# Second edge sum of a graph network: compare and multiply in one VectorE instruction per tile, in place of wide one-hots and ScalarE copies

## The chip, the cores and the metric

One NeuronCore of a Trainium2 chip runs the whole network in one launch. The metric is the device time of one execution in microseconds (us). The time before is the median of three runs.

## What is computed

The network has 6250 nodes with 256 features and 100000 edges, in two layers. Each layer adds a graph part and a mixer part and then a feed-forward part. The change touches the graph part of the second layer alone, an attention over edges:

```python
h = features @ W_layer.T + b_layer
a1 = (h @ w_a1.T + b_a1)[:, 0]
a2 = (h @ w_a2.T + b_a2)[:, 0]
row, col = indices
v = leaky_relu(a1[row] + a2[col], 0.01)
m = segment_max(v, row, n)
ev = exp(v - m[row])
s = segment_sum(ev, row, n)
out = segment_sum((ev / s[row])[:, None] * h[col], row, n)
```

## The kernel before, in words

The edges have been sorted by the row that they add to and are laid out in 880 tiles of 128 edges. Two tiles form a pair that belongs to one bucket of 128 rows, and 8 tiles (`T8`) form a batch, so that there are 110 batches (`NB`). For each edge `lane` holds its row's number within the bucket (0 to 127). For a tile, the 128x128 matrix with a 1 at (edge, lane of the edge) is its one-hot; multiplied with the gathered rows of `h` on TensorE it adds each edge's row to the right lane.

The class `Messages` holds the work on a batch n, as small functions for each engine:

- GpSimd, `pool_gather`: 8 indirect DMAs fetch the rows of `h` with the score a2 beside them into `g`, a ring of five batches (`GR`). From batch 5 on it waits until TensorE has summed the batch five before.
- VectorE, `dve_hold`: one instruction on 128x1024 elements compares the lane numbers with 0 to 127 and gives the batch's 8 one-hots in `one`, a ring of four. A small instruction on 128x8 then gives the shifted scores `a2s`; it waits for the gathered batch.
- ScalarE, `act_held`: 8 activations on 128x128 (Copy with a scale for each partition) multiply the one-hots by `a2s` and give `held`, of which there is one buffer.
- TensorE, `pe_turn`, two halves: transposes `held` into PSUM. ScalarE, `act_sign`, takes the sign of it (the transposed one-hot, for the lookup below), and VectorE, `dve_peak`, its maximum along the edges.
- VectorE, `dve_chain`: seven small instructions carry the maximum from pair to pair and give the row's m in two bf16 parts. ScalarE, `act_fade`, gives the factor by which the sum so far fades when m rises.
- TensorE, `pe_look`, looks a1 and m up for each edge. VectorE, `dve_exponents`, four small instructions, and ScalarE, `act_exp`, give `ev`.
- VectorE, `dve_weight`: one instruction on 128x1024 multiplies the one-hots in place by `ev`.
- TensorE, `pe_sum`, four pairs, and VectorE, `dve_add`, four times: `acc = acc * fade + sum` at the pair's bucket. The bucket's number is loaded into a register first (L1720), which has four small instructions of its own in VectorE's queue.

`forward_messages` weaves this into the second half of the mixer. Each engine goes through the same steps s; in step s VectorE holds batch s + 2, takes the peaks of batch s + 1, looks up and weights batch s and adds batch s - 1, all in the order that `step` writes out. There are 112 steps. In the first 100, four to a chunk of 250 rows, the mixer's own work on the chunk stands between as `first()` and `second()`; the last 12 hold the edges' work alone. GpSimd has nothing else to do than gather.

The order in VectorE's queue is this (L2067):

```python
            def step(s, first, second):
                ms.dve_hold(dve, s + 2)
                ms.dve_peak(dve, s + 1, 0)
                first()
                ms.dve_add(dve, s - 1, 0)
                ms.dve_add(dve, s - 1, 1)
                ms.dve_peak(dve, s + 1, 1)
                ms.dve_chain(dve, s + 1)
                second()
                ms.dve_exponents(dve, s)
                ms.dve_add(dve, s - 1, 2)
                ms.dve_weight(dve, s)
                ms.dve_add(dve, s - 1, 3)
```

The functions that the change touches, with `forward_messages`, follow.

Of the kernel before, what the change touches and what calls it, by code (L numbers as in the profile page):

```python
# [8 lines left out]
ALU = mybir.AluOpType  # L9
ACT = mybir.ActivationFunctionType  # L10
AX_X = mybir.AxisListType.X
ds = bass.ds
P = 128
# [28 lines left out]
class Phase:  # L42


    def __init__(self, nc, name):
        self.nc, self.name, self.ctx, self.sems = nc, name, ExitStack(), []
        self.loops, self.rings = [], []
# [5 lines left out]
    def sb(self, name, shape, dt=F32):  # L53
        return self.ctx.enter_context(self.nc.sbuf_tensor(f"{self.name}_{name}", shape, dt))
# [4 lines left out]
    def sem(self, name):  # L59
        s = self.nc.alloc_semaphore(f"{self.name}_{name}")  # L60
        self.sems.append(s)
        return s
# [99 lines left out]
PB = 4  # L162
NB = 110
# [1409 lines left out]

LOOK = 6
T8 = 2 * PB
HELD, ONES = 1, 4


class Messages:
# [5 lines left out]
    def __init__(self, nc, held, ctx, order, table_d):  # L1585
        def sb(name, shape, dt=F32, ctx=ctx):
            return ctx.enter_context(nc.sbuf_tensor(f"messages_{name}", shape, dt))
        self.nc, self.order, self.table_d = nc, order, table_d
        self.acc, self.ident, self.bucket = sb("acc", [P, HB, D + 1], ctx=held), sb("ident", [P, P], ctx=held), sb("bucket", [1, NPR], I32)
        self.lane, self.idx = sb("lane", [P, ST]), sb("idx", [P, ST], I32)  # L1590
        with ExitStack() as early:
            self.rec = sb("rec", [P, ST, 3], ctx=early)
        self.g = [sb(f"g{q}", [P, T8, D + 2]) for q in range(GR)]
        self.iota_t = sb("iota", [P, P])
        self.one = [sb(f"one{b}", [P, T8, P]) for b in range(ONES)]
        self.held = sb("held", [P, T8, P])
        self.heldT = [sb(f"heldT{b}", [P, T8, P], BF16) for b in range(2)]
        self.stays, self.a1_c, self.look = sb("stays", [P, NPR]), sb("a1_c", [P, NPR]), sb("look", [P, NPR, LOOK], BF16)
        self.best, self.m, self.shift = sb("best", [P, NPR + 1]), sb("m", [P, NPR + 1]), sb("shift", [P, 2])
        self.a2s, self.peak, self.mraw, self.m32, self.drop, self.fall = ([sb(f"{n}{b}", [P, w]) for b in range(2)] for n, w in (  # L1600
            ("a2s", T8), ("peak", PB), ("mraw", PB), ("m32", PB), ("drop", PB), ("fall", PB)))
        self.fade = [sb(f"fade{b}", [P, PB]) for b in range(3)]
        self.found, self.z, self.lz, self.d, self.ev = ([sb(f"{n}{b}", s) for b in range(2)] for n, s in (
            ("found", [P, T8, 2]), ("z", [P, T8]), ("lz", [P, T8]), ("d", [P, T8]), ("ev", [P, T8])))
        sem = lambda name: nc.alloc_semaphore(f"messages_{name}")
        self.loaded, self.ready = sem("loaded"), sem("ready")
        self.landed = [sem(f"landed{q}") for q in range(GR)]
        (self.onehot, self.shifted, self.held_s, self.hturned, self.signed, self.peaked, self.chained, self.raw, self.maxed, self.m_hi, self.m_mid,
         self.m_sum, self.dropped, self.fallen, self.faded, self.looked, self.read, self.zs, self.lzs, self.less, self.exped, self.weighted, self.summed,
         self.added) = (sem(n) for n in (  # L1610
             "onehot", "shifted", "held_s", "hturned", "signed", "peaked", "chained", "raw", "maxed", "m_hi", "m_mid",
             "m_sum", "dropped", "fallen", "faded", "looked", "read", "zs", "lzs", "less", "exped", "weighted", "summed", "added"))

    def banks(self, ph):
# [24 lines left out]
    def dve_hold(self, dve, n):  # L1639
        if not 0 <= n < NB:  # L1640
            return
        if n == 0:
            dve.wait_ge(self.ready, 2)
        if n >= ONES:
            dve.wait_ge(self.summed, (n - ONES + 1) * PB)
        self.nc.vector.tensor_tensor(self.one[n % ONES][:, :, :], self.iota_t[:, None, :].to_broadcast([P, T8, P]),
                                     self.lane[:, n * T8:(n + 1) * T8].unsqueeze(2).to_broadcast([P, T8, P]), ALU.is_equal).then_inc(self.onehot, 1)
        dve.wait_ge(self.landed[n % GR], (n // GR + 1) * (16 * T8))
        if n >= 2:
            dve.wait_ge(self.held_s, n - 1)  # L1650
        self.nc.vector.tensor_scalar(self.a2s[n % 2][:, :], self.g[n % GR][:, :, D + 1], self.shift[:, 0:1], 1.0, ALU.add, ALU.max).then_inc(self.shifted, 1)

    def dve_peak(self, dve, n, k):
        if not 0 <= n < NB:
# [53 lines left out]
    def dve_weight(self, dve, n):  # L1708
        if not 0 <= n < NB:
            return  # L1710
        one = self.one[n % ONES]
        dve.wait_ge(self.held_s, n + 1)
        dve.wait_ge(self.exped, n + 1)
        self.nc.vector.tensor_tensor(one[:, :, :], one[:, :, :], self.ev[n % 2][:, :].unsqueeze(2).to_broadcast([P, T8, P]), ALU.mult).then_inc(self.weighted, 1)  # L1714

    def dve_add(self, dve, n, k):
        if not 0 <= n < NB:
# [9 lines left out]
                                            ALU.mult, ALU.add).then_inc(self.added, 1)  # L1727

    def act_held(self, act, n):
        if not 0 <= n < NB:
            return
        act.wait_ge(self.onehot, n + 1)
        act.wait_ge(self.shifted, n + 1)
        if n:
            act.wait_ge(self.hturned, 2 * n)
        for j in range(T8):
            ins = self.nc.scalar.activation(self.held[:, j, :], self.one[n % ONES][:, j, :], ACT.Copy, scale=self.a2s[n % 2][:, j:j + 1])  # L1739
        ins.then_inc(self.held_s, 1)  # L1740

    def act_sign(self, act, n, k):
        if not 0 <= n < NB:
# [29 lines left out]
    def pe_turn(self, pe, n, k):  # L1773
        if not 0 <= n < NB:
            return
        if k == 0:
            pe.wait_ge(self.held_s, n + 1)
        if n or k:
            pe.wait_ge(self.peaked, 2 * n + k)
        for j in range(PB):  # L1780
            mm = self.nc.tensor.transpose(self.hT_ps[:, j * P:(j + 1) * P], self.held[:, k * PB + j, :], self.ident[:, :])  # L1781
        mm.then_inc(self.hturned, 1)

    def pe_look(self, pe, n):
# [98 lines left out]
def forward_messages(nc, name, span, ms, KH, KP, x_d, qT_d, mixer, out_d, c_d, gain_d, offset_d, w1_d, b1_d, w2_d, b2_d):  # L1883
# [7 lines left out]
    with SpanPhase(nc, name, span) as ph:  # L1891
# [114 lines left out]
        def _(act):  # L2006
# [6 lines left out]
            def step(s, first, second, reload=False):  # L2013
                ms.act_sign(act, s + 1, 0)
                first()
                ms.act_sign(act, s + 1, 1)
                ms.act_held(act, s + 2)
                second()
                if reload:
                    act.preload_act_table_set("natural_log_exp_and_others")  # L2020
                ms.act_fade(act, s + 1)
                ms.act_exp(act, s)

            for c in range(NCH):
                b, s = c % 2, STEPS * c - 2
# [1313 lines left out]
```

## Time and profile before

| | |
|---|---|
| median of 3 runs | 6689.16 us (6687.9 to 6704.43) |
| profiled execution, its own time | 6691.31 us |
| its span, first to last instruction | 6689.5 us |
| TensorE matmul busy | 5302.9 us, 79% |
| VectorE (DVE) busy | 3514.2 us, 53% |
| ScalarE (ACT) busy | 2890.8 us, 43% |
| GpSimd (POOL) busy | 3374.8 us, 50% |
| mean granted TensorE clock | 0.903 |

The span is cut into stages that follow one another. The shares above are means over all of them, so the question which engine bounds the kernel has to be asked of the stage that is changed. The second edge sum with the mixer's second half is the stage from about 5075 to 6292 us.

### The profile page before, as it was taken

Reading aid. Unit: us, or ns where it says so; the run is one execution under the profiler, and the core shown is the slowest. Engines: PE = TensorE matmul, PEld = TensorE weight load, DVE = VectorE, ACT = ScalarE, POOL = GpSimd, SP = SyncE. Lnnn points to the kernel's source line nnn. Section 1 sums busy time; section 2 is a strip of 40 time slices with the busy share of each in tenths; the row PEclk is TensorE's granted clock in tenths of the full one; section 3 lists DMA queues with packets and bytes.
Section 4 is the critical chain, followed back from the end, with each engine's and each line's share of the span. In section 5 each row is a group of like instructions: output and inputs, shape, how many; then the busy total and the mean of one; then the engine's idle time right before and its main releaser. Section 6 shows DMA issues by size and latency. Waiting matters only on the chain. (4 is left out here: it accounts for less than half of the span.)

```text
span 6689.5 us, 87639 instructions
## 1 busy us (share of the span) xinstructions
PE 5302.9 (79%) x25860; PEld 4453.1 (67%) x25860; DVE 3514.2 (53%) x8926; ACT 2890.8 (43%) x6920; POOL 3374.8 (50%) x3345
## 2 busy tenths in 40 slices
PE   6047997794388799887998528999967888887699
PEld 4045886683377688776887417888835666666588
DVE  4975666621137533375332434444466777777551
ACT  2223444441246555465554123333335555555344
POOL 0045555556646666466554645661023777777200
PEclk7578999897699899998999858999978999999799
DMA  4012222211234433344334352111032444444611
GB/s 115 25 43 67 48 48 52 71 44 23 66 95 134 116 96 92 93 133 117 92 89 92 94 154 62 34 33 32 27 93 76 110 112 112 111 110 106 90 41 34
DMA packets 423344, 532.32 MB, mean 80 GB/s; under 512 B 100344, under 2 KB 360922, under 8 KB 420570
## 3 DMA queue, kind: packets, MB, share of 16 engines
q1 hardware_dynamic: 287866, 289.80, 15.3%
q0 software_dynamic: 135008, 236.92, 14.9%
q8 instruction: 213, 3.49, 0.2%
q14 instruction: 257, 2.11, 0.1%
HBM read 411.61 MB, written 114.84 MB: 79 GB/s over the span
## 5 line engine op out<-in xcount | busy, mean ns | idle before, releaser
L236 POOL DMA_INDIRECT sorted_dst<-edges_record,edges_place x784 | 791.0, 1009 | 775.2 <-DMA sorted_dst<-edges_record,edges_place 328.6
L1634 POOL DMA_INDIRECT messages_g<-h_rows,messages_idx x880 | 917.2, 1042 | 444.5 <-issue 264.0
L267 POOL DMA_INDIRECT edges_g<-xn_rows,edges_idx x880 | 863.3, 981 | 505.8 <-issue 240.9
L236 POOL DMA_INDIRECT sorted_src<-edges_record,edges_place x784 | 779.0, 994 | 652.8 <-issue 207.4
L990 PE MATMUL forward_f_ps<-forward_out,forward_w 128*128 128x250 f32 x3200 | 737.0, 377 | 197.0 <-ACT forward_out L629 192.4
L990 PEld LDWEIGHTS forward_f_ps<-forward_out,forward_w 128*128 128x128 f32 x3200 | 611.4, 191 | 273.9 <-ACT forward_out L629 192.8
L1000 PE MATMUL forward_y_ps<-forward_w,forward_g 128*125 128x256 f32 x3200 | 722.7, 379 | 0.0
L1000 PEld LDWEIGHTS forward_y_ps<-forward_w,forward_g 128*125 128x125 f32 x3200 | 592.3, 187 | 84.9
L1803 PE MATMUL forward_s_ps<-messages_g,messages_one 128*128 128x257 f32 x1760 | 471.2, 413 | 129.8 <-DVE messages_one L1714 122.5
L1019 ACT ACTIVATE forward_g<-forward_f_ps,forward_b 128x250 f32<-128x250 f32 x800 | 331.8, 466 | 450.0 <-PE forward_f_ps L990 448.8
L1803 PEld LDWEIGHTS forward_s_ps<-messages_g,messages_one 128*128 128x128 f32 x1760 | 338.5, 202 | 209.8 <-DVE messages_one L1714 154.7
L294 ACT ACTIVATE edges_g<-edges_g,edges_rec 128x256 f32<-128x256 f32 x880 | 361.8, 498 | 193.4 <-DMA edges_g<-xn_rows,edges_idx 193.4
L2457 PE MATMUL experts_f_ps<-experts_tT,experts_w 128*128 128x250 f32 x1600 | 377.7, 378 | 0.0
L2466 PE MATMUL experts_y_ps<-experts_w,experts_g 128*125 128x256 f32 x1600 | 377.3, 379 | 0.0
L2670 DVE SCALAR_TENSOR_TENSOR experts_acc<-experts_y_ps,experts_comb,experts_acc 125x256 f32<-125x256 f32 x400 | 175.0, 479 | 302.3 <-PE experts_y_ps L2466 301.8
L2466 PEld LDWEIGHTS experts_y_ps<-experts_w,experts_g 128*125 128x125 f32 x1600 | 299.4, 187 | 43.4
L2457 PEld LDWEIGHTS experts_f_ps<-experts_tT,experts_w 128*128 128x128 f32 x1600 | 295.7, 191 | 40.4 <-issue 8.4
L1748 ACT ACTIVATE messages_heldT<-forward_hT_ps 128x512 bf16<-128x512 f32 x220 | 130.0, 591 | 416.1 <-PE forward_hT_ps L1781 414.7
L1019 ACT ACT_TABLE_LOAD x100 | 128.3, 1283 | 372.5 <-PE forward_f_ps L990 372.5
L1726 DVE SCALAR_TENSOR_TENSOR messages_acc<-messages_acc,messages_fade,forward_s_ps 128x257 f32 x440 | 211.0, 480 | 139.0 <-issue 72.5
L606 DVE RECIPROCAL forward_rstd<-forward_dev 125x2 f32<-125x2 f32 x100 | 16.6, 166 | 506.5 <-ACT forward_dev L595 506.5
L1739 ACT ACTIVATE messages_held<-messages_one,messages_a2s 128x128 f32<-128x128 f32 x880 | 267.6, 389 | 0.0
(459 smaller groups left out, 10660.0 us busy)
## 6 DMA issues: line engine op xcount, KB each, us to landing
mix_rows<-forward_y SPq DMA_DIRECT2D x125, 250.0 KB
qT<-attend_qT SPq DMA_DIRECT2D x100, 250.0 KB, 3.1
forward_q<-qT SPq DMA_DIRECT2D x100, 250.0 KB
attend_x<-mix_rows SPq DMA_DIRECT2D x75, 250.0 KB
forward_xin<-mix_rows SPq DMA_DIRECT2D x75, 250.0 KB
edges_g<-xn_rows,edges_idx POOLq DMA_INDIRECT x880, 3.7
messages_g<-h_rows,messages_idx POOLq DMA_INDIRECT x880
sorted_dst<-edges_record,edges_place POOLq DMA_INDIRECT x784
```

The costliest lines, as they stand in the source:

```text
L236: self.nc.gpsimd.indirect_dma_start(self.orders[s][0], bass.IndirectOffsetOnAxis(self.place[s][:, j:j + 1], 0), self.record[s][:, j, :], N ...
L267: self.nc.gpsimd.indirect_dma_start(self.g[n % GR][:, j, 0:D], None, self.table_d, bass.IndirectOffsetOnAxis(self.idx[:, t:t + 1], 0)).the ...
L294: ins = self.nc.scalar.activation(self.g[n % GR][:, j, 0:D], self.g[n % GR][:, j, 0:D], ACT.Copy, scale=self.rec[:, t:t + 1, 2])
L990: mm = nc.tensor.matmul(f_ps[m][:, h * CW:(h + 1) * CW], w1[:, k, g0:g0 + P], ln.out[b][:, k, :], start=(k == 0), stop=(k == 1))
L1000: mm = nc.tensor.matmul(yps[:, t, :], g[b][:, m, t * TT:(t + 1) * TT], w2[:, m, :], start=(m == 0), stop=(m == FG - 1))
L1019: last = nc.scalar.activation(g[b][:, 2 * m + h, :], f_ps[m][:, h * CW:(h + 1) * CW], ACT.Gelu, bias=b1[:, 2 * m + h:2 * m + h + 1])
L1634: self.nc.gpsimd.indirect_dma_start(self.g[n % GR][:, j, :], None, self.table_d, bass.IndirectOffsetOnAxis(self.idx[:, t:t + 1], 0)).then_inc(
L1726: self.nc.vector.scalar_tensor_tensor(self.acc[:, ds(h, 1), :], self.acc[:, ds(h, 1), :], self.fade[n % 3][:, k:k + 1], self.s_ps[u % 2][: ...
L1739: ins = self.nc.scalar.activation(self.held[:, j, :], self.one[n % ONES][:, j, :], ACT.Copy, scale=self.a2s[n % 2][:, j:j + 1])
L1803: mm = self.nc.tensor.matmul(self.s_ps[u % 2][:, 0:D + 1], self.one[n % ONES][:, 2 * k + t, :], self.g[n % GR][:, 2 * k + t, 0:D + 1], sta ...
L2457: mm = nc.tensor.matmul(f_ps[n % 3][:, h * CW:(h + 1) * CW], w1[:, e, k, h * P:(h + 1) * P], tT[c % 2][:, k, :], start=(k == 0), stop=(k = ...
L2466: mm = nc.tensor.matmul(yps[m % 2][:, j, :], g[n % 4][:, k, j * TT:(j + 1) * TT], w2[:, e, k, :], start=(k == 0), stop=(k == 1))
```

## The change

The one-hots and the ScalarE copies go. VectorE's `tensor_scalar` takes the numbers 0 to 127, compares them with one number for each partition (the lane) and multiplies the outcome by a second (the score or the weight), both in one instruction, for one tile of 128x128 at a time. `held` is made so in `dve_hold` (8 instructions, after `a2s`, for which VectorE now waits on itself), and the weighted one-hots are made so in `dve_weight` (8 instructions, from nothing). `act_held` is dropped. `held` has two buffers now, and `one` two in place of four; `dve_weight` waits until the sums two batches before are done.

```diff
-HELD, ONES = 1, 4
+ONES = 2
...
-        self.held = sb("held", [P, T8, P])
+        self.held = [sb(f"held{b}", [P, T8, P]) for b in range(2)]
...
         if n == 0:
             dve.wait_ge(self.ready, 2)
-        if n >= ONES:
-            dve.wait_ge(self.summed, (n - ONES + 1) * PB)
-        self.nc.vector.tensor_tensor(self.one[n % ONES][:, :, :], self.iota_t[:, None, :].to_broadcast([P, T8, P]),
-                                     self.lane[:, n * T8:(n + 1) * T8].unsqueeze(2).to_broadcast([P, T8, P]), ALU.is_equal).then_inc(self.onehot, 1)
         dve.wait_ge(self.landed[n % GR], (n // GR + 1) * (16 * T8))
         if n >= 2:
             dve.wait_ge(self.held_s, n - 1)
         self.nc.vector.tensor_scalar(self.a2s[n % 2][:, :], self.g[n % GR][:, :, D + 1], self.shift[:, 0:1], 1.0, ALU.add, ALU.max).then_inc(self.shifted, 1)
+        dve.wait_ge(self.shifted, n + 1)
+        if n >= 2:
+            dve.wait_ge(self.hturned, 2 * (n - 1))
+        for j in range(T8):
+            t = n * T8 + j
+            ins = self.nc.vector.tensor_scalar(self.held[n % 2][:, j, :], self.iota_t[:, :], self.lane[:, t:t + 1], self.a2s[n % 2][:, j:j + 1], ALU.is_equal, ALU.mult)
+        ins.then_inc(self.held_s, 1)
...
-        one = self.one[n % ONES]
-        dve.wait_ge(self.held_s, n + 1)
+        if n >= ONES:
+            dve.wait_ge(self.summed, (n - ONES + 1) * PB)
         dve.wait_ge(self.exped, n + 1)
-        self.nc.vector.tensor_tensor(one[:, :, :], one[:, :, :], self.ev[n % 2][:, :].unsqueeze(2).to_broadcast([P, T8, P]), ALU.mult).then_inc(self.weighted, 1)
+        for j in range(T8):
+            t = n * T8 + j
+            ins = self.nc.vector.tensor_scalar(self.one[n % ONES][:, j, :], self.iota_t[:, :], self.lane[:, t:t + 1], self.ev[n % 2][:, j:j + 1], ALU.is_equal, ALU.mult)
+        ins.then_inc(self.weighted, 1)
...
-    def act_held(self, act, n):
-        if not 0 <= n < NB:
-            return
-        act.wait_ge(self.onehot, n + 1)
-        act.wait_ge(self.shifted, n + 1)
-        if n:
-            act.wait_ge(self.hturned, 2 * n)
-        for j in range(T8):
-            ins = self.nc.scalar.activation(self.held[:, j, :], self.one[n % ONES][:, j, :], ACT.Copy, scale=self.a2s[n % 2][:, j:j + 1])
-        ins.then_inc(self.held_s, 1)
...
-            mm = self.nc.tensor.transpose(self.hT_ps[:, j * P:(j + 1) * P], self.held[:, k * PB + j, :], self.ident[:, :])
+            mm = self.nc.tensor.transpose(self.hT_ps[:, j * P:(j + 1) * P], self.held[n % 2][:, k * PB + j, :], self.ident[:, :])
...
                 ms.act_sign(act, s + 1, 1)
-                ms.act_held(act, s + 2)
                 second()
```

VectorE's queue, from the weighting of one batch over the end of a step to the first peak of the next, in the kernel before:

```order
L1714 TENSOR_TENSOR messages_one0<-messages_one0,messages_ev0 128x1024
L1720 TENSOR_LOAD messages_bucket
L1720 ISA x2
L1726 ISA
L1726 SCALAR_TENSOR_TENSOR messages_acc<-messages_acc,messages_fade0,forward1_s_ps1 128x257
L1646 TENSOR_TENSOR messages_one3<-messages_iota,messages_lane 128x1024
L1651 TENSOR_SCALAR messages_a2s1<-messages_g2,messages_shift 128x8
L1659 TENSOR_REDUCE messages_peak0<-forward1_hT_ps 128x2
```

The same place after the change:

```order
L1719 TENSOR_SCALAR messages_one1<-messages_iota,messages_lane,messages_ev1 128x128 x8
L1726 TENSOR_LOAD messages_bucket
L1726 ISA x2
L1732 ISA
L1732 SCALAR_TENSOR_TENSOR messages_acc<-messages_acc,messages_fade2,forward1_s_ps1 128x257
L1647 TENSOR_SCALAR messages_a2s0<-messages_g1,messages_shift 128x8
L1653 TENSOR_SCALAR messages_held0<-messages_iota,messages_lane,messages_a2s0 128x128 x8
L1662 TENSOR_REDUCE messages_peak1<-forward1_hT_ps 128x2
```

Each of the two wide instructions has become eight short ones, and the eight that make `held` stand behind `a2s` and ahead of the peak, where the wide comparison stood ahead of `a2s`.

ScalarE's queue in the second of the four steps of a chunk (`forward1_g` is the mixer's gelu, L2032 to L2020 the two table loads around it), before:

```order
L1748 ACTIVATE messages_heldT0<-forward1_hT_ps 128x512
L1739 ACTIVATE messages_held<-messages_one1,messages_a2s1 128x128 x8
L2032 ACTIVATE forward1_g<-forward1_f_ps1,forward1_b1 128x250 x2
L2020 ACT_TABLE_LOAD
L1757 ACTIVATE messages_fall0<-messages_drop0 128x4
L1761 ACTIVATE messages_fade0<-messages_fall0 128x4
```

And after:

```order
L1743 ACTIVATE messages_heldT1<-forward1_hT_ps 128x512
L2026 ACTIVATE forward1_g<-forward1_f_ps1,forward1_b1 128x250 x2
L2014 ACT_TABLE_LOAD
L1752 ACTIVATE messages_fall1<-messages_drop1 128x4
L1756 ACTIVATE messages_fade1<-messages_fall1 128x4
```

The eight copies ahead of the gelu are gone, and nothing takes their place.

## Rows read from the trace of the kernel before

**Rows 1.** Busy us of each engine by stretch, second edge sum (windows view)

```profile
core 0: us, PE busy (x) PEld busy (x) DVE busy (x) ACT busy (x) POOL busy (x), PEclk, DMA share, GB/s
5000.00:5075.00 75.00, 54.16 (x286) 31.46 (x284) 43.19 (x188) 30.78 (x113) 0.00 (x0) 0.80 0.24 73
5600.00:5800.00 200.00, 167.21 (x928) 136.49 (x927) 154.14 (x420) 115.73 (x314) 154.89 (x149) 0.97 0.42 110
```

**Rows 2.** GpSimd's gathers one by one (timeline: start us, us, engine, line, [idle before])

```profile
5616.21 0.95 POOL L1634 DMA_INDIRECT messages_g<-h_rows,messages_idx  x1 [0.30 <-issue]
...
5619.97 1.72 POOL L1634 DMA_INDIRECT messages_g<-h_rows,messages_idx  x1 [0.30 <-issue]
...
5623.52 1.07 POOL L1634 DMA_INDIRECT messages_g<-h_rows,messages_idx  x1 [0.31 <-issue]
```

**Rows 3.** VectorE's waits, 5090 to 6129 us (waits view: total us, times, longest)

```profile
DVE messages_acc L1726 <- issue: 66.7, 91, 1.5
DVE messages_a2s L1651 <- DMA messages_g<-h_rows,messages_idx: 47.9, 28, 2.8
DVE messages_one L1714 <- ACT messages_ev L1769: 29.3, 47, 1.2
```

**Rows 4.** VectorE at the first and last one-hot of the body (timeline)

```profile
5089.92 1.22 DVE L1646 TENSOR_TENSOR messages_one<-messages_iota,messages_lane 128x1024 f32<-128x1024 f32 x1
...
6129.09 1.22 DVE L1646 TENSOR_TENSOR messages_one<-messages_iota,messages_lane 128x1024 f32<-128x1024 f32 x1
```

**Rows 5.** VectorE's wait for gathers, 6129 to 6295 us (waits view)

```profile
DVE messages_a2s L1651 <- DMA messages_g<-h_rows,messages_idx: 31.1, 11, 4.4
```

**Rows 6.** VectorE from one weighting to the next step's first adds (timeline)

```profile
5618.42 0.17 DVE L1706 TENSOR_TENSOR messages_d<-messages_lz,messages_found 128x8 f32<-128x8 f32 x1
...
5619.25 0.48 DVE L1726 SCALAR_TENSOR_TENSOR messages_acc<-messages_acc,messages_fade,forward_s_ps 128x257 f32 x1 [0.67 <-issue]
5619.65 1.22 DVE L1714 TENSOR_TENSOR messages_one<-messages_one,messages_ev 128x1024 f32<-128x1024 f32 x1
...
5620.79 0.47 DVE L1726 SCALAR_TENSOR_TENSOR messages_acc<-messages_acc,messages_fade,forward_s_ps 128x257 f32 x1
...
5621.18 1.22 DVE L1646 TENSOR_TENSOR messages_one<-messages_iota,messages_lane 128x1024 f32<-128x1024 f32 x1
...
5622.32 0.22 DVE L1651 TENSOR_SCALAR messages_a2s<-messages_g,messages_shift 128x8 f32<-128x8 f32 x1
5622.45 0.68 DVE L1659 TENSOR_REDUCE messages_peak<-forward_hT_ps 128x2 f32<-128x512 f32 x1
5623.05 0.72 DVE L612 TENSOR_SCALAR forward_nrm<-forward_x,forward_mv,forward_rstd 125x256 f32<-125x256 f32 x2
5623.69 0.47 DVE L1726 SCALAR_TENSOR_TENSOR messages_acc<-messages_acc,messages_fade,forward_s_ps 128x257 f32 x1
```

**Rows 7.** Two tensor_scalar of 128x128 with one number per partition (timeline)

```profile
5071.89 0.48 DVE L2086 TENSOR_SCALAR forward_diag<-messages_ident,forward_b 128x128 f32<-128x128 f32 x2 [4.78 <-DMA forward_w<-in_L_mix_W]
```

**Rows 8.** Durations of tensor_scalar (min/median/max ns, first and last start, shape)

```profile
L2086 DVE TENSOR_SCALAR forward_diag<-messages_ident,forward_b x2: 280/283/286, 5071.9 to 5072.1; 128x128 f32<-128x128 f32 x2
L1866 DVE TENSOR_SCALAR prepare_is_bucket<-prepare_bucket_f,prepare_number x1: 431/431/431, 4893.1 to 4893.1; 49x440 f32<-49x440 f32 x1
L612 DVE TENSOR_SCALAR forward_nrm<-forward_x,forward_mv,forward_rstd x250: 394/409/639, 658.9 to 6098.5; 125x256 f32<-125x256 f32 x125
```

**Rows 9.** The same L612 in all stages, then in 5075 to 6300 us (lines: xcount | busy us, mean ns)

```profile
L612 DVE TENSOR_SCALAR forward_nrm<-forward_x,forward_mv,forward_rstd 125x256 f32<-125x256 f32 x250 | 95.8, 424 | 4.2 <-DVE forward_rstd L606 0.6
...
L612 DVE TENSOR_SCALAR forward_nrm<-forward_x,forward_mv,forward_rstd 125x256 f32<-125x256 f32 x48 | 17.4, 404 | 0.0
```

**Rows 10.** ScalarE through the second half of a step with gelu (timeline)

```profile
5634.65 2.43 ACT L1739 ACTIVATE messages_held<-messages_one,messages_a2s 128x128 f32<-128x128 f32 x8
5636.98 0.81 ACT L2032 ACTIVATE forward_g<-forward_f_ps,forward_b 128x250 f32<-128x250 f32 x2
5637.81 1.28 ACT L2020 ACT_TABLE_LOAD   x1
...
5639.45 0.19 ACT L1769 ACTIVATE messages_ev<-messages_d 128x8 f32<-128x8 f32 x1
```

More of the change, by code:

```diff
@@ L1607, in __init__ @@
         self.landed = [sem(f"landed{q}") for q in range(GR)]
-        (self.onehot, self.shifted, self.held_s, self.hturned, self.signed, self.peaked, self.chained, self.raw, self.maxed, self.m_hi, self.m_mid,
+        (self.shifted, self.held_s, self.hturned, self.signed, self.peaked, self.chained, self.raw, self.maxed, self.m_hi, self.m_mid,
          self.m_sum, self.dropped, self.fallen, self.faded, self.looked, self.read, self.zs, self.lzs, self.less, self.exped, self.weighted, self.summed,
          self.added) = (sem(n) for n in (
-             "onehot", "shifted", "held_s", "hturned", "signed", "peaked", "chained", "raw", "maxed", "m_hi", "m_mid",
+             "shifted", "held_s", "hturned", "signed", "peaked", "chained", "raw", "maxed", "m_hi", "m_mid",
              "m_sum", "dropped", "fallen", "faded", "looked", "read", "zs", "lzs", "less", "exped", "weighted", "summed", "added"))
```

## The prediction

> **What bounds the kernel now.** The busy shares of the whole span tell nothing here, so I began with the windows view of the stage that is changed. From 5600 to 5800 us no engine is full by its busy time: TensorE has 167.21 us of 200, VectorE 154.14, GpSimd 154.89 [rows 1]. GpSimd is full all the same. Between two of its gathers stand 0.30 us of issue [rows 2], and 149 gathers with as many gaps give 154.9 + 44.7 = 199.6 us of 200. A batch is 8 gathers, so one comes every 8 x 200 / 149 = 10.74 us.
>
> Next I looked for whoever stands right behind it. VectorE makes its one-hot once in a step: the one at 5089.92 and the one at 6129.09 are 96 steps apart [rows 4], 1039.2 us or 10.82 us a step. I call this the body. In it VectorE waits 47.9 us for gathered rows [rows 3], and without that wait it would need 1039.2 - 47.9 = 991.3 us, 10.33 us a step. What else it waits for is mostly its own: 66.7 us ahead of the adds are "issue" [rows 3], the loading of the bucket's number. So VectorE has half a microsecond to spare in a step, no more. In the last 12 steps, to about 6292 us, it waits another 31.1 us for gathers [rows 5]. That is all the slack that there is against the change: 79 us.
>
> ScalarE is the loosest of the four, at 115.73 us of 200 [rows 1]. The change takes work from it and gives work to VectorE.
>
> **What goes from VectorE.** The comparison of 1024 elements: from its start at 5621.18 to the peak's at 5622.45, the small `a2s` included, 1.27 us. The multiplication: from 5619.65 to the next add at 5620.79, 1.14 us [rows 6]. Together 2.41 us a step.
>
> **What comes to VectorE.** Sixteen `tensor_scalar` of 128x128 with two numbers per partition, a form that the trace does not show. Two rows stand on either side of it. With one number per partition and the same 128x128, a pair takes 0.48 us [rows 7] at 283 ns each [rows 8], so that the second starts 0.20 us after the first. With two numbers, but 256 elements, a pair takes 0.72 us [rows 6] at 409 ns each [rows 8]: 0.31 us. The elements cost little: 440 of them took 431 ns and 128 took 283 [rows 8], that is 148 ns for 312 elements, so 128 more cost 0.06 us (the first has 49 partitions and the second 128, which I take to make no difference). Taking these from 0.31 leaves 0.25; I take 0.26 us, nearer to the row with two numbers, since the second number is what the other lacks. The ends are 0.20 and 0.31. Sixteen times 0.26 are 4.16 us. Ahead of the eight for `held` VectorE now waits for its own `a2s`: 0.22 us [rows 6] and some 0.05 for the signal, 0.27. That is 4.43 us, and the balance is 4.43 - 2.41 = +2.02 us a step.
>
> **Who gets in the way.** The same L612 takes 404 ns in this stage and 424 over all stages, 639 at most [rows 8, 9]; I put the 20 ns down to gathers or scatters that hold something which VectorE wants. In this stage it falls at a fixed moment between gathers, and the sixteen new ones will fall anywhere. 16 x 20 ns = 0.32 us, for the share of time in which GpSimd works (10.0 of 12.3 us): +0.26. The ends are 0 and 0.32.
>
> **What comes back.** VectorE waits 29.3 us in the body for ScalarE's exponents [rows 3]. There the eight copies, 2.43 us, push the gelu to 5636.98, the table load behind it to 5637.81 and the exponent to 5639.45 [rows 10]. Without the copies all of this comes up to 2.4 us sooner, more than the longest of those waits, and the weighting starts later besides. I credit the whole, 29.3 / 96 = -0.31 us a step. The rest of ScalarE's relief I put at nothing, since VectorE's own queue covers it. The second buffer of `held` and the shorter ring of `one` are at nothing too: sums two batches back were added by VectorE itself a step earlier.
>
> **What GpSimd does.** A gather takes 0.95 us, but 1.72 at 5619.97 [rows 2], while the multiplication of 5619.65 to 5620.87 runs [rows 6], and 1.07 beside the pair of L612 at 5623.05. The wide ones go, so a batch needs between 8 x 1.25 = 10.0 and some 10.7 us. Either way it is under what VectorE then needs, and GpSimd waits for the sums.
>
> **The sum.** 2.02 + 0.26 - 0.31 = +1.97 us a step. The body: 991.3 + 96 x 1.97 = 1180.4 us in place of 1039.2, +141. The last 12 steps lose the wait of 31.1 and gain 12 x 2.28 = 27.4: -4. The start: two batches held ahead, 2 x 1.0 us more, against one block of copies of 2.43 less ahead of the first transpose: nothing. In all +138 us on the profiled execution's own 6691.3: **6829 us**. The median of the three runs shown is 6689.2, two below it; I leave that out. VectorE's step is then 12.3 us, and VectorE is the bound.
>
> **The rivals.**
>
> *The load of the bucket's number shows.* The wide multiplication hid the register load for the last add of a step. Behind a short instruction it takes 0.83 us from that one's start to the add (5618.42 to 5619.25, 0.67 of it idle). If the last of the eight were followed so, it would cost 0.83 - 0.26 = 0.57 us a step, 108 x 0.57 = 62: 6891 us. Against it: behind the pair of L612 at 5623.05 the add starts at 5623.69, at once, so the queue runs ahead over at least two short ones [rows 6]. 14%.
>
> *GpSimd stays the bound, through blocked gathers.* If a gather cannot slip in between two short instructions, it waits for the end of the eight. They fill 4.2 of 12.3 us, so 2.7 of 8 gathers fall in them and wait 1.0 us on the mean: 10.0 + 2.8 = 12.8 us a step, 0.5 above VectorE's, 96 x 0.5 = 48 more: 6877 us. It decides from 12.3 us a batch on. For it speaks the gather of 1.72 us, against it that of 1.07, which ran into two short ones in a row and lost only 0.12. 10%. The Trainium skill, "SBUF — State Buffer", section "Who interferes with whom", has VectorE and GpSimd share a pair of ports, which a VectorE instruction in a two-port mode or with two SBUF inputs holds for its whole length; by that rule each short one can hold up a gather, and the trace agrees as far as the 1.72 goes.
>
> *The short ones are cheap, and GpSimd gets free.* At 0.13 us each VectorE would need 10.33 + 0.27 + 16 x 0.13 - 2.41 - 0.31 = 9.96 us, and with the wide instructions gone a batch of gathers takes some 10.3: 96 x (10.3 - 10.82) = -50: 6641 us, **faster**. It decides from an interval of about 0.15 us down. The pair of rows 7 speaks against it, with 0.20 at one number. 5%. The Trainium skill, "VectorE: DVE Perf Modes", section "The TRN2 errata — SBUF-src ops pay a fixed extra latency per instruction", has a table by which such an instruction costs 58 + 128/2 = 122 cycles at 0.96 GHz, an estimate of 0.127 us, and the sum would end at this rival's time; the same section says that the table is too low and measured some 150 cycles in place of 58, an estimate of 0.22 us. The trace disagrees with the first and has 0.20 to 0.31 us.
>
> *The slack takes nearly all.* At 0.20 us each and with nothing in the way, VectorE gains 3.20 + 0.27 - 2.41 - 0.31 = 0.75 us a step: 991.3 + 72.0 - 1039.2 = +24, and the last steps give 12 x 1.06 - 31.1 = -18: 6697 us, no change. It needs the second number to be free. 8%.
>
> **How the numbers follow.** The forecast has 63%, the rivals 14, 10, 5 and 8. Its own low end: 0.23 us an instruction and no hindrance, 3.68 + 0.27 - 2.41 - 0.31 = +1.23 us a step, +70 in the body and -13 behind it: 6748. The high end is the first rival's 6891 and a little for TensorE's clock: it was granted 0.97 while TensorE was busy 167 of 200 us, and 0.80 at 54 of 75 [rows 1]. After the change TensorE is busy some 73%, and a transposition between two peaks may take 0.1 us longer, 11 us in all: 6902. I give 6750 to 6900; it leaves out the two cheap cases and some of the far end. A measurement can tell about 0.3%, 20 us, from no change. Faster 5%, same 8%, slower 87%.
>
> **What would show it.** VectorE's `messages_held` and `messages_one` 880 times each at about 0.34 us, starting 0.26 apart; its wait for gathers gone, a step of 12.3 us; its busy time in a 200 us stretch up from 154 to about 165; GpSimd waiting for `forward_s_ps` some 2 us a batch, its gathers at 0.95 to 1.2 us; no wait for `messages_ev`. If the short ones start 0.20 apart, or if VectorE still waits for gathers in the body, the sum is wrong, and if an idle time of over 0.3 us stands ahead of the fourth add, the first rival holds.

## The result and the profile after

The change makes the kernel slower: 6801.15 us (median of 4 runs, 6795.51 to 6821.25) against 6694.15 us (median of 4 runs), or +107 us. The medians stand as 1.0160 to 1; the ratio on record, estimated over the same runs, is 1.0172 (95% interval 1.0155 to 1.0188). The forecast was 6829 us, +138. The profiled execution of the change has a span of 6795.7 us, 106.2 more than that of before.

The windows view of the changed kernel, for the stretch that [rows 1] shows of before, and for its body (batch 2's `a2s` to batch 98's, the same 96 steps):

```profile
5600.00:5800.00 200.00, 157.43 (x830) 126.06 (x828) 167.73 (x607) 69.29 (x151) 126.49 (x133) 0.93 0.38 100
5083.10:6227.27 1144.17, 887.07 (x4784) 712.81 (x4783) 969.05 (x3477) 398.61 (x868) 719.66 (x755) 0.96 0.38 99
```

The third pair of numbers behind the length is VectorE: 167.73 us of 200, up from 154.14 [rows 1]. ScalarE has fallen from 115.73 to 69.29 and GpSimd from 154.89 to 126.49. The body is 1144.2 us in place of 1039.2: 11.92 us a step in place of 10.82.

The waits of VectorE and then of GpSimd in the body, which answer to [rows 3]:

```profile
DVE messages_acc L1732 <- issue: 57.8, 81, 1.5
DVE messages_acc L1732 <- DVE messages_acc L1732: 25.3, 95, 0.7
DVE messages_acc L1732 <- PE forward_s_ps L1798: 24.6, 37, 0.7
DVE messages_a2s L1647 <- DMA messages_g<-h_rows,messages_idx: 11.2, 15, 1.3
DVE messages_peak L1662 <- ACT messages_heldT L1743: 10.8, 25, 0.9
DVE messages_one L1719 <- ACT messages_ev L1764: 2.2, 4, 0.6
...
POOL messages_g L1634 <- PE forward_s_ps L1798: 366.0, 95, 162.1
```

The wait for the exponents has gone from 29.3 us to 2.2, that for gathers from 47.9 to 11.2. GpSimd now waits for the sums before nearly every batch, 366.0 us less the one start of 162.1. The bound has moved from GpSimd to VectorE.

The new instructions in the timeline of VectorE, the place of [rows 6]:

```profile
5616.11 2.13 DVE L1719 TENSOR_SCALAR messages_one<-messages_iota,messages_lane,messages_ev 128x128 f32<-128x128 f32 x8
5618.16 0.47 DVE L1732 SCALAR_TENSOR_TENSOR messages_acc<-messages_acc,messages_fade,forward_s_ps 128x257 f32 x1
5618.55 0.22 DVE L1647 TENSOR_SCALAR messages_a2s<-messages_g,messages_shift 128x8 f32<-128x8 f32 x1
5618.81 2.29 DVE L1653 TENSOR_SCALAR messages_held<-messages_iota,messages_lane,messages_a2s 128x128 f32<-128x128 f32 x8
5620.87 0.68 DVE L1662 TENSOR_REDUCE messages_peak<-forward_hT_ps 128x2 f32<-128x512 f32 x1
```

Eight take 2.05 us from their start to what follows (5616.11 to 5618.16), 0.256 us each; over all 192 rows of eight in the body the mean is 2.06, and one starts 0.257 us after the other. The forecast had 0.26. The add behind them starts at once, so the load of the bucket's number stays hidden. `a2s` to the first of the eight is 0.26 us (0.27 forecast). A step of VectorE's own work has thus grown by 2 x 2.05 + 0.26 - 2.41 = 1.95 us.

The lines view of GpSimd's gathers in the bodies, of the kernel before and then of the changed one (busy us, mean ns, idle us before):

```profile
L1634 POOL DMA_INDIRECT messages_g<-h_rows,messages_idx x753 | 787.0, 1045 | 398.5 <-issue 226.5 <-PE forward_s_ps L1803 172.0
```

```profile
L1634 POOL DMA_INDIRECT messages_g<-h_rows,messages_idx x736 | 701.8, 954 | 558.2 <-PE forward_s_ps L1798 360.1 <-issue 198.1
```

A gather takes 954 ns on the mean in place of 1045. The short instructions hinder it less than the wide ones did.

Where the 106.2 us of span come from: the body +105.0, the last steps +7.6 (from batch 98's `a2s` to the last add 169.4 us in place of 161.8), the first two held batches -2.6, and -3.9 in stages that the change does not touch.

The last steps, as windows and then as VectorE's waits, of the kernel before and then of the changed one:

```profile
6130.22:6291.98 161.76, 107.59 (x479) 80.26 (x477) 100.94 (x272) 50.52 (x161) 90.70 (x87) 0.79 0.60 74
DVE messages_a2s L1651 <- DMA messages_g<-h_rows,messages_idx: 31.1, 11, 4.4
DVE messages_acc L1726 <- PE forward_s_ps L1803: 9.8, 14, 1.6
DVE messages_peak L1659 <- ACT messages_heldT L1748: 3.7, 8, 0.6
```

```profile
6227.27:6396.67 169.40, 110.77 (x484) 84.89 (x483) 126.12 (x455) 22.34 (x65) 81.07 (x86) 0.77 0.55 70
DVE messages_acc L1732 <- PE forward_s_ps L1798: 13.4, 15, 1.9
DVE messages_peak L1662 <- ACT messages_heldT L1743: 9.7, 13, 1.0
DVE messages_a2s L1647 <- DMA messages_g<-h_rows,messages_idx: 6.2, 4, 1.8
```

### The profile page after: what moved, and what is told of

It is laid out like the page before. It is cut to its first block and busy times, and to the rows that moved or that the text cites. A ratio compares the mean times of both kernels' runs of the same rounds, so it can differ in the third digit from the quotient of the medians.

```text
span 6795.7 us, 88296 instructions
## 1 busy us (share of the span) xinstructions
PE 5307.6 (78%) x25860; PEld 4450.0 (65%) x25860; DVE 3717.7 (55%) x10466; ACT 2642.0 (39%) x6040; POOL 3295.2 (48%) x3345
## 5 line engine op out<-in xcount | busy, mean ns | idle before, releaser
L1634 POOL DMA_INDIRECT messages_g<-h_rows,messages_idx x880 | 840.0, 955 | 623.4 <-PE forward_s_ps L1798 385.4
L1798 PE MATMUL forward_s_ps<-messages_g,messages_one 128*128 128x257 f32 x1760 | 485.5, 423 | 184.9 <-DVE messages_one L1719 178.7
L305 PE MATMUL attend_s_ps<-edges_g,edges_one 128*128 128x257 f32 x800 | 212.4, 388 | 68.2 <-issue 59.7
```

The lines of the kernel that those rows point to most:

```text
L305: mm = self.nc.tensor.matmul(s_ps[u % 2][:, 0:D + 1], self.one[n % 2][:, 2 * k + t, :], self.g[n % GR][:, 2 * k + t, :], start=(t == 0), s ...
L1634: self.nc.gpsimd.indirect_dma_start(self.g[n % GR][:, j, :], None, self.table_d, bass.IndirectOffsetOnAxis(self.idx[:, t:t + 1], 0)).then_inc(
L1798: mm = self.nc.tensor.matmul(self.s_ps[u % 2][:, 0:D + 1], self.one[n % ONES][:, 2 * k + t, :], self.g[n % GR][:, 2 * k + t, 0:D + 1], sta ...
```

## Experiments

Each run is compared with the kernel before on the same chip. Beside the ratio I give the body, measured as above from the profile, since it holds the mechanism without the other stages. The first eight runs were on two chips where the kernel before takes 6732 and 6729 us, the last four on one where it takes 7331. On the first two the body starts 28 to 45 us later than in the two traces above, about as much as these chips cost in all (38 and 35 us), so I set their bodies against 1039.2 and 1144.2. It remains a comparison of single executions on different chips, for no trace of the kernel before was taken there.

**The fused weighting alone.** In the kernel before, L1714 becomes eight short ones:

```diff
-        self.nc.vector.tensor_tensor(one[:, :, :], one[:, :, :], self.ev[n % 2][:, :].unsqueeze(2).to_broadcast([P, T8, P]), ALU.mult).then_inc(self.weighted, 1)
+        for j in range(T8):
+            t = n * T8 + j
+            ins = self.nc.vector.tensor_scalar(one[:, j, :], self.iota_t[:, :], self.lane[:, t:t + 1], self.ev[n % 2][:, j:j + 1], ALU.is_equal, ALU.mult)
+        ins.then_inc(self.weighted, 1)
```

> The kernel before, with its wide one-hots and ScalarE copies kept; only the weighting is made of eight fused short instructions. Theory A (the price is VectorE's own time, 0.257 us a short instruction, against half a microsecond of slack behind GpSimd): the weighting takes 2.05 us in place of 1.14, VectorE needs 10.33 + 0.91 = 11.24 us a step, GpSimd's wait goes, the body of 96 steps grows by about 40 us, the last steps by nothing; about 6730 us, 1.005 of before. Theory B (the loss sits in the part made for held: the wait of VectorE on its own a2s, the place ahead of the peak): no change, within 10 us of before. Theory C (short ones and gathers hinder each other): short ones over 0.30 us apart, over 6760 us.

Measured 1.0057 (1.004 to 1.0074). Its body, and its waits for exponents and gathers:

```profile
5119.44:6202.39 1082.94, 907.74 (x4787) 737.65 (x4786) 878.23 (x2805) 615.04 (x1636) 759.44 (x756) 0.93 0.40 105
```

```profile
DVE messages_one L1716 <- ACT messages_ev L1772: 27.3, 45, 1.2
...
DVE messages_a2s L1651 <- DMA messages_g<-h_rows,messages_idx: 4.3, 10, 0.8
```

The body grew by 43.7 us where theory A has 40: 96 x 0.91 = 87 us more of VectorE's own work, less the wait for gathers, which fell from 47.9 us to 4.3. The place ahead of the peak (theory B) isn't needed for a loss.

**One number in place of two.** In the changed kernel the second factor is the constant 1.0, in both loops; the scaling is left out.

```diff
-            ins = self.nc.vector.tensor_scalar(self.held[n % 2][:, j, :], self.iota_t[:, :], self.lane[:, t:t + 1], self.a2s[n % 2][:, j:j + 1], ALU.is_equal, ALU.mult)
+            ins = self.nc.vector.tensor_scalar(self.held[n % 2][:, j, :], self.iota_t[:, :], self.lane[:, t:t + 1], 1.0, ALU.is_equal, ALU.mult)
...
-            ins = self.nc.vector.tensor_scalar(self.one[n % ONES][:, j, :], self.iota_t[:, :], self.lane[:, t:t + 1], self.ev[n % 2][:, j:j + 1], ALU.is_equal, ALU.mult)
+            ins = self.nc.vector.tensor_scalar(self.one[n % ONES][:, j, :], self.iota_t[:, :], self.lane[:, t:t + 1], 1.0, ALU.is_equal, ALU.mult)
```

> The change, with a constant 1.0 in place of the score and of the weight as second factor, so that the scaling is left out. Theory A: the short ones start 0.20 us apart as in the pair with one number, 16 x 0.057 = 0.91 us less a step, 11.0 us a step in place of 11.92, 96 x 0.91 = 87 less in the body and some 5 to 10 in the last steps: about 6705 us. If a second number costs nothing and 0.257 is the price of the compare and multiply in one or of fast repetition, or if another engine sets the step: no change, 6800 us.

Measured 1.0103 (1.0086 to 1.012). Body, short instructions and wait:

```profile
5117.87:6224.10 1106.23, 893.86 (x4783) 719.57 (x4783) 884.48 (x3477) 399.98 (x868) 720.92 (x755) 0.95 0.39 102
```

```profile
5681.52 1.72 DVE L1653 TENSOR_SCALAR messages_held<-messages_iota,messages_lane 128x128 f32<-128x128 f32 x8
5683.16 0.68 DVE L1662 TENSOR_REDUCE messages_peak<-forward_hT_ps 128x2 f32<-128x512 f32 x1
```

```profile
DVE messages_a2s L1647 <- DMA messages_g<-h_rows,messages_idx: 39.2, 22, 2.6
```

Eight take 1.64 us here (5681.52 to 5683.16) and 1.60 on the mean of the body's 192 rows of eight, 0.200 each. In the changed kernel they take 2.06, so the second number costs 0.057 us an instruction. But the body fell by 38 us and not by 87, and VectorE waits 39.2 us for gathers, though GpSimd needs only 8 x (0.95 + 0.30) = 10.0 us a batch of a step of 11.5. That was a miss, and asked for a cause.

**The same with six buffers for gathered rows.** `g` and its semaphores have 6 in place of `GR`'s 5, in `Messages` alone.

```diff
+MR = 6
...
-        self.g = [sb(f"g{q}", [P, T8, D + 2]) for q in range(GR)]
+        self.g = [sb(f"g{q}", [P, T8, D + 2]) for q in range(MR)]
...
-        if n >= GR:
-            pool.wait_ge(self.summed, (n - GR + 1) * PB)
+        if n >= MR:
+            pool.wait_ge(self.summed, (n - MR + 1) * PB)
```

> The run with the constant second factor (e3), with six buffers for the gathered rows in place of five. In e3 the short ones started 0.20 us apart as expected, 0.91 us a step less, but the step fell by 0.40 only and VectorE waited 39 us for gathers. Theory D (the ring of five is a bound of its own, a gather starts only when the sums five batches before are done, and lands 15 us later): with six the wait goes, the step falls to 11.0 us, the body to about 1057 us, 1.004 of before. If something else takes the time (GpSimd's rate, the landing of the data), the wait stays and so do e3's 1.010.

Measured 1.0002 (0.9987 to 1.0018); the body:

```profile
5128.17:6181.70 1053.53, 882.75 (x4784) 712.83 (x4783) 881.83 (x3477) 398.57 (x868) 721.78 (x755) 0.96 0.41 107
```

10.97 us a step where 11.0 was expected, and VectorE's wait for gathers is gone. So the ring of five is a bound of its own (theory D): GpSimd may start a batch only after the sums five batches back, and from its first gather to the `a2s` that waits for the batch the run with five buffers shows 15.8 us on the mean (22 batches), though GpSimd works only 10.0 of them.

**Seven gathers a batch, in the kernel before and in the changed one.** The eighth tile's rows are left out from batch 5 on.

```diff
-        for j in range(T8):
+        for j in range(T8 if n < GR else T8 - 1):
...
-        dve.wait_ge(self.landed[n % GR], (n // GR + 1) * (16 * T8))
+        dve.wait_ge(self.landed[n % GR], 16 * T8 + n // GR * (16 * (T8 - 1)))
```

> The kernel before, with seven gathers a batch in place of eight from the sixth batch on (the eighth tile's rows are left out, the tile keeps old ones). Theory A (GpSimd bounds the kernel before and VectorE stands half a microsecond behind it): VectorE sets the step at 10.33 us, the body falls by its 48 us of waits and the last steps by some 15 to 30: about 6620 us. If GpSimd is not what bounds before (the wait for gathers is only the landing of data or the wait of VectorE for itself), the time falls by under 15 us.

> The changed kernel, with seven gathers a batch in place of eight from the sixth batch on (the eighth tile's rows are left out). Theory A (VectorE sets the step of the changed kernel, GpSimd waits for it): the body loses at most the 11 us that VectorE still waits for gathers, the last steps some 5: 6785 to 6800 us. Theory C (gathers hinder the short instructions): an eighth fewer gathers takes an eighth of the hindrance and the waits, and the step falls visibly, by over 25 us.

The kernel before falls to 0.9902 (0.9882 to 0.9921), the changed one stands at 1.0131 (1.0114 to 1.0148). The bodies:

```profile
5127.52:6127.11 999.59, 864.85 (x4788) 708.22 (x4787) 791.38 (x2133) 614.13 (x1636) 683.34 (x662) 0.97 0.39 101
```

```profile
5119.08:6260.02 1140.94, 905.46 (x4784) 725.42 (x4783) 968.55 (x3477) 399.18 (x868) 629.27 (x661) 0.94 0.34 88
```

Without an eighth of its gathers the kernel before loses 39.6 us of its body, where theory A has 48, and stands at 10.41 us a step; the changed kernel loses 3.2. GpSimd bounded the one and does not bound the other. The changed kernel's ratio fell by more than its body, 0.4%; 6.8 us more lie in the last steps (162.6 us in place of 169.4), and the rest isn't accounted for by the edit.

**ScalarE's copies put back.** The changed kernel with eight activations where `act_held` stood, from constants into a spare tile.

```diff
+    def act_spare(self, act, n):
...
+        act.wait_ge(self.shifted, n + 1)
+        for j in range(T8):
+            self.nc.scalar.activation(self.spare[:, j, :], self.iota_t[:, :], ACT.Copy, scale=self.stays[:, j:j + 1])
...
                 ms.act_sign(act, s + 1, 1)
+                ms.act_spare(act, s + 2)
                 second()
```

> The changed kernel, with eight copies of 128x128 put back into ScalarE's queue where the old ones stood; they read constants and write a spare tile that nobody reads. Theory A: ScalarE's exponents come late again in the two gelu steps of a chunk, VectorE waits some 0.38 us a step for them as before, 96 x 0.38 = 36 us more than the change: about 1.023 of before. If ScalarE's relief was worth nothing to the changed kernel, it stays at 1.017.

Measured 1.0199 (1.017 to 1.0228). Body, and the wait for exponents:

```profile
5122.97:6298.78 1175.82, 918.28 (x4790) 735.77 (x4789) 971.69 (x3477) 616.19 (x1639) 718.63 (x756) 0.93 0.37 96
```

```profile
DVE messages_one L1720 <- ACT messages_ev L1772: 31.7, 45, 0.9
```

The intervals of the two ratios overlap, so the times alone don't tell the two kernels apart. The body is 31.6 us longer, 0.33 a step, and in it the wait is back at 31.7 us from 2.2, which accounts for 29.5. ScalarE's relief was worth what VectorE had waited for it, no more.

**Wide multiplication on VectorE.** In the kernel before, the copies are replaced by one wide instruction.

```diff
+        self.nc.vector.tensor_tensor(self.held[n % 2][:, :, :], self.one[n % ONES][:, :, :],
+                                     self.a2s[n % 2][:, :].unsqueeze(2).to_broadcast([P, T8, P]), ALU.mult).then_inc(self.held_s, 1)
...
-                ms.act_held(act, s + 2)
```

> The kernel before, with ScalarE's eight copies replaced by a third wide VectorE multiplication (one-hots times scores, 1.14 us), held with two buffers. Theory A: the fixed price of sixteen short ones is what the change pays, so three wide ones cost less: VectorE 10.33 + 1.14 + 0.14 - 0.38 = 11.2 us a step, GpSimd, held up by three wide ones in place of two, 11.1: the body 1075 to 1085 us, about 1.006 of before. If taking the work from ScalarE to VectorE is what costs, whatever the form, it comes out near the change's 1.017.

Measured 1.0095 (1.0069 to 1.0121), body and wait:

```profile
5131.70:6239.44 1107.74, 875.38 (x4786) 706.29 (x4787) 903.69 (x2229) 398.55 (x865) 805.02 (x754) 0.97 0.39 102
```

```profile
DVE messages_a2s L1651 <- DMA messages_g<-h_rows,messages_idx: 27.2, 22, 2.9
```

The order is right, the size not: the body is 23 to 33 us over the expected. VectorE is busy 903.69 us, 65 less than in the change, but waits 27.2 us for gathers; without that wait the body would be 1080.5, as expected. A gather takes 1069 ns here, and the ring has five buffers; which of the two makes the wait isn't shown. The form costs: three wide ones do what sixteen short ones do, for half the loss.

**Weighting on ScalarE.** In the kernel before, `dve_weight` goes and ScalarE multiplies behind its exponents.

```diff
+        for j in range(T8):
+            ins = self.nc.scalar.activation(one[:, j, :], one[:, j, :], ACT.Copy, scale=self.ev[n % 2][:, j:j + 1])
+        ins.then_inc(self.weighted, 1)
...
                 ms.act_exp(act, s)
+                ms.act_weight(act, s)
```

> The kernel before, with the weighting taken from VectorE's wide multiplication and given to ScalarE as eight copies with a scale behind its exponents. VectorE needs 10.33 - 1.14 - 0.31 = 8.9 us a step, GpSimd is held up by one wide instruction in place of two, 10.35 us a batch. Theory A: GpSimd stays the bound and the step is 10.4 us, 38 us less: 0.994 of before. Rival: ScalarE then has 8.6 us of work a step in one chain with the exponents, and in gelu steps 10.8, so that it becomes the bound: the step 10.8 to 11.3 us, no change or up to 1.007.

Measured 1.0077 (1.0052 to 1.0101), body and VectorE's longest wait:

```profile
5125.82:6215.93 1090.12, 905.39 (x4784) 747.80 (x4783) 700.91 (x2037) 841.88 (x2399) 751.43 (x754) 0.92 0.40 104
```

```profile
DVE messages_peak L1659 <- ACT messages_heldT L1750: 112.9, 131, 2.1
```

The rival held, a little beyond its upper end (11.36 us a step). ScalarE, 77% busy, has the signs for the peaks behind its eight copies, and VectorE, with 90 us less to do, waits 112.9 us for them.

**Six buffers in the changed kernel.** The same edit of the ring as in the run with one number and six buffers.

> The changed kernel with six buffers for the gathered rows in place of five. Theory D (the ring of five is a bound that begins to hold VectorE up as soon as a step comes near 11 to 12 us): the 11 us of waits in the body go and some 5 to 10 us of the last steps, 1.014 to 1.015 of before in place of 1.017; VectorE's own 11.8 us a step stay. If it is VectorE alone: no change.

Measured 1.0109 (1.0062 to 1.0157) on the last chip. VectorE's longest waits in the body:

```profile
DVE messages_acc L1733 <- issue: 93.2, 143, 2.8
DVE messages_acc L1733 <- PE forward_s_ps L1799: 65.0, 36, 3.8
```

It waits for no gather any more, but the body is 1255.2 us, longer than on the other chips. Ahead of the adds it waits 93.2 us of "issue" and 65.0 for TensorE, in place of 57.8 and 24.6. The ratio can't be set against 1.0172, and how much of it the ring gave stays open.

**Inputs of the wide instructions in PSUM.** In the kernel before, the numbers 0 to 127 and `ev` lie in free columns of the lookup's bank; the second run has six buffers besides, the third ScalarE's copies in two halves.

```diff
+        self.iota_p, self.ev = self.look_ps[:, 384:512], [self.look_ps[:, 256 + 64 * b:256 + 64 * b + T8] for b in range(2)]
...
-        self.nc.vector.tensor_tensor(self.one[n % ONES][:, :, :], self.iota_t[:, None, :].to_broadcast([P, T8, P]),
+        self.nc.vector.tensor_tensor(self.one[n % ONES][:, :, :], self.iota_p[:, None, :].to_broadcast([P, T8, P]),
```

> The kernel before, with its two wide VectorE instructions and ScalarE copies as they are, but the numbers 0 to 127 and the exponents lie in PSUM, in free columns of the lookup's bank, so that each wide instruction has one input in SBUF in place of two. Theory E (a wide instruction with two SBUF inputs holds gathers up, 0.1 us of 1.045 on the mean, and so makes GpSimd the bound): gathers at 0.95 us, a batch 10.0 us, VectorE's own 10.33 us sets the step, the body 1000 us in place of 1039, the last steps 5 to 15 less: 0.992 of before. If the long gathers come from something else (the landing, the descriptors), or if the wide ones get slower from PSUM: 1.000 or above.

> The run before this one with six buffers for the gathered rows. Theories D and E together: no wait for gathers, 10.33 us a step, the body 991 us, the last steps 10 us shorter: 0.990 of before. If the ring of five does nothing at this pace: the same as the run with five.

> The run before this one, with ScalarE's eight copies in two halves: four where they stood, four behind the exponents. Theory A: the exponents come 1.2 us sooner in the gelu steps, VectorE's wait of 0.31 us a step for them falls by half or more, 10.1 us a step, the body 15 to 20 us less: 0.987 of before. Rival: the second half of held comes late for the next step's transposes, VectorE waits for the peaks instead: no gain, or up to 10 us lost.

Measured 1.0056 (1.0022 to 1.009), 1.0086 (1.0053 to 1.012) and 1.0076 (1.0039 to 1.0112), where 0.992, 0.990 and 0.987 were expected: none is faster, and all three are misses. From the run with six buffers: the gathers, the body, and one chunk's stretch by stretch (the second number from the end but two is the granted TensorE clock):

```profile
L1637 POOL DMA_INDIRECT messages_g<-h_rows,messages_idx x758 | 719.9, 950 | 669.4 <-PE forward_s_ps L1807 407.8 <-issue 203.1 <-remote 58.5
```

```profile
5605.54:6831.65 1226.11, 961.12 (x4787) 751.27 (x4786) 790.99 (x2133) 611.90 (x1636) 718.93 (x757) 0.90 0.35 93
6105.00:6113.50 8.50, 4.44 (x26) 2.74 (x24) 5.26 (x17) 5.92 (x16) 3.78 (x4) 0.88 0.25 63
6113.50:6117.50 4.00, 3.94 (x10) 3.10 (x11) 3.86 (x10) 0.00 (x0) 2.86 (x4) 0.50 0.38 99
```

The first half of theory E is shown. The same two wide instructions, with VectorE's busy time unchanged (790.99 us against 792 in the same stretch of before) but one SBUF input each, leave a gather at 950 ns in place of 1045. One by one, in the body: in the kernel before the 271 gathers that overlap a wide instruction take 1.20 us on the mean, up to 1.98, and the other 483 take 0.96. With the inputs in PSUM the 273 that overlap one take 0.945, at most 0.968. The other runs fall in line: 1.07 us on the mean over all gathers with three such wide instructions a step, 1.00 to 1.01 with one, 0.95 with none.

The second half, the time, is not shown. VectorE waits for other things on this chip (the first two lines stand in place of 66.7 and 20.9 us in before; there the signs took 9.6, and nothing was put down to "remote", by which the profile names no engine of this core):

```profile
DVE messages_acc L1730 <- issue: 112.4, 163, 2.4
DVE messages_acc L1730 <- PE forward_s_ps L1807: 64.0, 25, 3.4
DVE messages_peak L1663 <- ACT messages_heldT L1752: 71.1, 47, 4.3
DVE messages_found L1700 <- remote: 64.0, 25, 4.0
```

GpSimd in turn waits for the sums. The clock granted to TensorE is 0.90 over the body, where the kernel before had 0.97 on its own chip. In the stretch at 6105 us TensorE is busy 4.44 us of 8.5; in the next four microseconds the clock is 0.50, the lower level of 1.2 GHz, and eight matmuls of the sums take 3.79 us, where eight at 6120 us take 1.98. What makes the steps longer isn't shown: it may be the chip, as in the run before these, but that the inputs in the lookup's bank have a price of their own, beside the gathers, isn't ruled out. No trace of the kernel before was taken on this chip, so it also stays open whether its relief would pay on the others. No version that beats both kernels has been shown.

## Why the prediction was right, and where its sum was off

The direction and the mechanism held: GpSimd bounded the kernel before and VectorE stood just behind it (the run with seven gathers); VectorE's time rose past both and sets the step now. The measured time lies within the range, 28 us under the forecast. Term by term, a step:

- *The short instruction*: 0.26 us taken, 0.257 measured. The second number, 0.06 in the interpolation, costs 0.057 by its own run; the price of the elements has no run of its own. The balance of +2.02 us came out at 1.95.
- *What comes back from ScalarE*: -0.31 taken. VectorE's wait for the exponents fell by 27.1 us, 0.28 a step, and the copies put back cost 0.33.
- *Who gets in the way*: +0.26 taken, some 0.02 measured (2.06 us for eight on the mean, 2.05 at the median). **This is the term that failed.** The 20 ns were there, but in the wrong place. Of the 1536 short ones in the body of the changed kernel, the 255 that start 0.4 to 0.6 us after the start of a gather last 0.46 us on the mean, up to 0.586; the others last 0.34. The mean of all, 0.363, is 22 ns over their median. But in both groups the next one starts 0.257 us later. I had read a longer duration as a later start of the next.
- *The ring of five* was not in the sum: I had GpSimd wait for the sums and took that to be free. It left VectorE 11.2 us of waits for gathers in the body, by the prediction's own words a sign that the sum was wrong, and with 0.057 us off each short instruction it was a bound of its own.
- *The last steps*: -4 us forecast, +7.6 measured. VectorE's wait for gathers did nearly vanish there, from 31.1 us to 6.2, and its busy time grew by 25.2, so these two balance. The rest came from waits that the sum did not have: 6.0 us more for ScalarE's signs ahead of the peaks and 3.6 more for the sums.

The body was forecast 36 us too long. The hindrance carries 0.26 x 96 = 25 us of it and the balance 7; the exponents go 2 and the ring 11 the other way. The remaining 18 are small: 9 us less of "issue" ahead of the adds, and some 7 less for adds, peaks and the small ones. Their cause is open.

The hindrance of L612, from which I took the 20 ns, stands at the same place. In the kernel before:

```profile
2705.25 0.98 POOL L267 DMA_INDIRECT edges_g<-xn_rows,edges_idx  x1 [1.93 <-DMA sorted_src<-edges_record,edges_place]
2705.70 0.95 DVE L612 TENSOR_SCALAR forward_nrm<-forward_x,forward_mv,forward_rstd 125x256 f32<-125x256 f32 x2
```

The pair starts 0.45 us after a gather and takes 0.95 us where the pair of [rows 6] takes 0.72. So there the second was late too. In the stage at hand none of the 48 lasts over 410 ns. Why a row of eight short ones takes up the delay of one isn't shown.

Of the rivals, the shown load of the bucket's number did not come (the fourth add starts 2.05 us after the first of eight, with no idle time ahead of it). The blocked gathers did not come either: 954 ns on the mean, not 1.3 us. That speaks on the rule of the Trainium skill, "SBUF — State Buffer", section "Who interferes with whom". As far as a two-input instruction goes, the trace and the PSUM runs agree with it (1.20 us beside one, 0.945 with one input in PSUM), though the same section infers that a `tensor_tensor` leaves the making of a DMA's descriptors alone; by the measured 1.20 us it does not leave a gather alone. A short one in a row of eight costs a gather 0.01 us on the mean, so such a row does not hold the ports as one instruction would. The table of the Trainium skill, "VectorE: DVE Perf Modes", section "The TRN2 errata — SBUF-src ops pay a fixed extra latency per instruction", gives 58 + 64 cycles, an estimate of 0.127 us, half of the 0.257 measured and under two thirds of the 0.200 with one number. The 150 cycles of the same section, an estimate of 0.22 us, lie between the two.

## What to carry to other kernels

A fused instruction saves a pass over the elements, but a wide instruction split by tile pays a price per tile: here 16 x 0.257 us for what two instructions of 1.14 us and eight copies on an engine with time to spare had done. Before moving work, find the second engine behind the bound and how far it stands behind: 0.5 us of 10.8 was all the room, and ScalarE's 2.43 us of saved work gave back 0.33. A longer duration in a row is not yet a later start of the next instruction: read the interval where it can be read. And a ring counts as a bound as soon as the engine that fills it waits for its emptying.

## What the runs showed of the hardware

- A second per-partition number costs a `tensor_scalar` of 128x128 0.057 us (0.200 to 0.257 us from start to start, in rows of eight).
- Two wide VectorE instructions with both inputs in SBUF lengthen an indirect gather from 950 to 1045 ns on the mean, and one that overlaps them to 1.20 us, up to 1.98; with one input of each in PSUM they take as long themselves (1.22 us) and the gathers stay at 950.
- Of two-number instructions back to back, one that starts 0.4 to 0.6 us after the start of a gather lasts 0.46 us in place of 0.34, but the next is not late for it; the gathers lose about 0.01 us.
